# A four-layer gated kernel: routing and first weight loads moved within the first attention, and the shift of x moved to ScalarE in the competitive attention

## The chip, the cores and the metric

The kernel runs on one core of a Trainium2 chip. The metric is the device time of one execution in microseconds (us), as the median of several runs. A profile is the record of one such execution.

## What is computed

Four layers, each x + tanh(gate) * attention(layernorm(x), ctx), followed by x + tanh(gate) * ffn(layernorm(x)), over x of 32 batches x 128 rows x 128 and ctx of 32 x 77 x 128. The attention and the ffn differ from layer to layer. The change touches three of the eight:

```
# layer 0, attention: 16 heads, softmax over the 77 context rows
out = softmax(Q @ K.T / sqrt(8)) @ V @ Wo + bo
# layer 0, ffn: 2 of 8 experts for each row
probs = softmax(xf @ router_w.T); topv, topi = top_k(probs, 2); topv = topv / topv.sum()
out = sum over the two experts e: topv[e] * (gelu(xf @ w1[e]) @ w2[e])
# layer 1, attention: each row goes to its best context row
sim = sigmoid(beta + alpha * C @ X.T); mask = one_hot(argmax over context rows)
agg = (sim * mask) @ X + C; denom = mask.sum(rows) + 1.0
out = X + sim.T @ (agg / denom)
```

In the last line X is layernorm(x), so layer 1 adds gate * (X + ...) to x.

## The kernel before

The program is a row of phases (`nc.Block`), with a barrier of all engines between two. Within a phase each engine runs its own list of instructions in the order of the code, and semaphores tie the lists. Four arrays stay in SBUF throughout: x (32 batches, 128 rows on the partitions), its moments, the context and its transpose.

**`head_attention`, layer 0.** A software pipeline `pipeline4` over the 32 batches: in one step one batch is in its front (transposes, projections), another in its middle (exp, sum, scaling), another in its back (transposes of the probabilities, product with V), another in its tail (statistics of the new x). Per step VectorE sums the exponentials (L608), takes the reciprocal (L611, `softmax_recip`), and GpSimd scales 4 x 4 heads with it (L439), on which TensorE's transposes wait. Once 12 of the first 16 batches are through, the same phase routes the first half (16 batches) of the layer's own ffn beside the attention, in unrolled steps: moments and normalisation of x to `r.xn` in four groups of four batches (L576, at the `NORMALISE_STEPS` 15, 16, 17 and 19), their transposes on TensorE (L693), logits, exp at step 21 (`EXP`), `pick_first` and `pick_second` (top two experts), counts on TensorE, `rank_pairs` (place of each row in its expert's list), `slots_of_pairs`, `weigh_experts`, `expert_of_tiles` (which expert each tile of sorted rows belongs to). From step 25 (`SCATTER`) GpSimd issues, ahead of its scaling, three indirect DMAs a step (L431) that scatter 128 rows each into `sorted_x` in DRAM. There are 32, and those left go out in the last step, after its scaling. SP loads later weights and clears the scratch in this phase (to L410).

**`sparse_experts`, layer 0.** The sorted rows come in 2 halves of 20 tiles of 256 rows. SP loads for each tile two blocks of 256 KB of up weights (L926, L927, `load_weights`; the expert's number is read from `r.expert`) and 128 KB of rows (L935, `load_rows`) into buffers that are six deep (`DEPTH`); the first three tiles' weights come first, then the first three tiles' rows. TensorE transposes the rows (L1179) and multiplies. Within the phase GpSimd scatters the second half's rows (L964), and the second half's loads wait for that.

**`competitive_attention`, layer 1.** Eight groups of four batches run through a pipeline of front, middle and back. ScalarE normalises the next group (L1392, four activations), copies its transpose (L1402), exponentiates (L1407, L1410) and copies the transposed sims (L1398). VectorE takes the reciprocal that ends the sigmoid (L1452), counts and averages the rows of the group before (L1458 to L1465), finds the best context row of each row (L1470 to L1477, products and reductions over 128x308) and updates x (L1482). GpSimd weighs the tokens (L1356), multiplies xn by the gate (L1360) and adds that to x (L1364). Beside it the second half of the layer 0 ffn is brought home: GpSimd gathers rows of `sorted_y` (L1346), three batches a step, and VectorE adds them to x with their weights (`combine`, L1429 and L1434). TensorE runs the aggregation (L1504), transposes the sims (L1509), transposes the next xn (L1515), takes the similarities (L1521) and the output (L1529).

The helper `chain` links VectorE's instructions by a semaphore; `MID` and `BACK` count its links in a step. `clear` has GpSimd reset the semaphores of the phase before.

## Time and profile before

| | us |
|---|---|
| median of three runs (lowest, highest) | 1668.2 (1667.2, 1670.81) |
| the profiled execution's own time | 1669.93 |
| its span | 1668.1 |
| first attention, as cut below | 238.40 (23.00 to 261.40) |
| expert phase, layer 0 | 191.20 (261.40 to 452.60) |
| competitive attention | 103.90 (452.60 to 556.50) |

Over the span TensorE is busy 1395.9 us, VectorE 1056.0, GpSimd 789.5 and ScalarE 695.9; TensorE's mean granted clock is 0.922 of full speed. The profile page gives these sums, the chain of waits and the costliest groups of instructions. The trace behind it can be asked for windows (busy time of each engine in a stretch), for groups by line, and for the timeline (each instruction with its start, its length and what released it). In all of them PE is TensorE, PEld its weight loads, DVE is VectorE, ACT is ScalarE, POOL is GpSimd, and SPq, ACTq, POOLq are those engines' DMA queues. "L431" is a line of the kernel, and names are those of the program's buffers.

### The profile page before, as it was taken

To read this page: it belongs to the slowest core of one execution; us is meant where nothing else is said; L and a number is where in the kernel's file an instruction comes from. 1 tells how busy PE (TensorE), PEld (TensorE's weight loads), DVE (VectorE), ACT (ScalarE), POOL (GpSimd) and SP (SyncE) were. 2 spreads that over 40 slices of the span, in tenths; PEclk is the share of its full clock that TensorE was granted. 3 is DMA by queue.
4 is the path that set the end of the run, shared out by engine and by line. 5 is a ranking of instruction groups with operands and counts; after the bars stand their busy time and mean duration, and the time that the engine had idled before them with its cause. 6 is when DMAs were issued, how large, how long until landed. Compare 5 with 4: busy or idle time off the path is not lost. (4 is left out here: it accounts for less than half of the span.)

```text
span 1668.1 us, 34024 instructions
## 1 busy us (share of the span) xinstructions
PE 1395.9 (84%) x10919; PEld 1117.9 (67%) x10919; DVE 1056.0 (63%) x2354; ACT 695.9 (42%) x1695; POOL 789.5 (47%) x1005
## 2 busy tenths in 40 slices
PE   4999774989656785999979986999999999687996
PEld 3777554989645454666645555787888787486984
DVE  4888761413389696999958883555565755263455
ACT  3676452323344332665544442445545544321121
...
DMA packets 96485, 100.02 MB, mean 60 GB/s; under 512 B 12149, under 2 KB 69677, under 8 KB 95726
## 3 DMA queue, kind: packets, MB, share of 16 engines
...
## 5 line engine op out<-in xcount | busy, mean ns | idle before, releaser
L439 POOL TENSOR_TENSOR exp_scores<-exp_scores,softmax_recip 128x308 f32<-128x308 f32 x256 | 181.9, 743 | 180.7 <-DVE softmax_recip L611 180.6
L633 PE MATMUL psum<-identity,exp_scores 128*77 128x128 f32 x1024 | 163.6, 285 | 38.8 <-POOL exp_scores L439 26.2
L1944 POOL TENSOR_TENSOR exp_scores_xattn<-exp_scores_xattn,softmax_recip_xattn 128x1640 f32<-128x1640 f32 x32 | 93.5, 2923 | 162.4 <-DVE softmax_recip_xattn L2117 162.4
L1201 PE MATMUL psum<-sorted_transposed_ffn,tile_weights_up_ffn 128*128 128x128 f32 x1280 | 165.7, 284 | 5.3 <-DVE sorted_transposed_ffn L1089 5.2
L633 PEld LDWEIGHTS psum<-identity,exp_scores 128*77 128x77 f32 x1024 | 122.1, 152 | 61.9 <-issue 29.4
L1201 PEld LDWEIGHTS psum<-sorted_transposed_ffn,tile_weights_up_ffn 128*128 128x128 f32 x1280 | 155.1, 198 | 12.2 <-DVE sorted_transposed_ffn L1089 11.6
L975 POOL DMA_INDIRECT gathered_rows_ffn<-sorted_y,slot_ffn x96 | 90.9, 947 | 105.7 <-DMA sorted_y<-expert_rows_ffn 47.1
L454 ACT COPY probs_transposed<-psum 77x512 f32<-77x512 f32 x192 | 111.3, 582 | 57.3 <-PE psum L633 55.3
L964 POOL DMA_INDIRECT sorted_x<-xn_ffn,slot_ffn x64 | 61.5, 961 | 141.2 <-DVE slot_ffn L851 122.4
L1211 PE MATMUL psum<-expert_weights_down_ffn,hidden_ffn 128*128 x960 | 124.5, 281 | 3.4 <-issue 2.9
L1211 PEld LDWEIGHTS psum<-expert_weights_down_ffn,hidden_ffn 128*128 128x128 f32 x960 | 116.8, 197 | 5.3 <-issue 5.2
L1993 ACT ACTIVATE exp_scores_xattn<-psum,scaled_negated_max_xattn 128x205 f32<-128x205 f32 x256 | 106.6, 451 | 0.0
L2184 PE MATMUL psum<-kv_transposed_xattn,queries_xattn 128*128 128x205 f32 x512 | 97.8, 346 | 3.4 <-DVE queries_xattn L2122 3.4
L1004 ACT ACTIVATE hidden_ffn<-psum 128x512 f32<-128x512 f32 x80 | 47.7, 597 | 119.0 <-PE psum L1201 119.0
L536 DVE TENSOR_REDUCE negated_max<-psum 128x16 bf16<-128x1232 f32 (+1 forms) x64 | 90.8, 1419 | 4.5 <-PE psum L668 4.5
L2184 PEld LDWEIGHTS psum<-kv_transposed_xattn,queries_xattn 128*128 128x128 f32 x512 | 90.8, 196 | 4.0 <-DVE queries_xattn L2122 3.9
L1971 ACT COPY kv_transposed_xattn<-psum 128x205 f32<-128x205 f32 x32 | 10.6, 332 | 191.5 <-PE psum L2197 191.5
L1733 POOL TENSOR_TENSOR pick_ffn<-pick_ffn,descending_count 128x512 f32<-128x512 f32 x32 | 52.4, 1638 | 73.8 <-DVE pick_ffn L1800 73.8
L1089 DVE COPY sorted_transposed_ffn<-psum 128x256 f32<-128x256 f32 x80 | 33.7, 421 | 81.5 <-PE psum L1179 81.4
L2064 DVE TENSOR_REDUCE negated_max_xattn<-psum 128x4 f32<-128x820 f32 x64 | 64.7, 1011 | 25.3 <-PE psum L2184 24.9
L1119 DVE COPY expert_rows_ffn<-psum 128x256 f32<-128x256 f32 x80 | 34.0, 425 | 73.0 <-PE psum L1211 68.3
L502 ACT ACTIVATE exp_scores<-psum 128x1232 f32<-128x1232 f32 x64 | 76.7, 1198 | 6.1 <-PE psum L704 3.3
...
## 6 DMA issues: line engine op xcount, KB each, us to landing
...
sorted_x<-xn_ffn,slot_ffn POOLq DMA_INDIRECT x128, 2.2
gathered_rows_ffn<-sorted_y,slot_ffn POOLq DMA_INDIRECT x128, 2.7
```

Source lines behind the costliest of these rows:

```text
L439: nc.gpsimd.tensor_tensor(e[:, par, heads, :], e[:, par, heads, :], rec.to_broadcast([S, HG, KC]), ALU.mult).then_inc(s["probs_ready"], 1)
L454: nc.scalar.copy(pt[:, g * HG:(g + 1) * HG, :], m.psum[0:KC, 4 + g % 2, :].rearrange("p (h s) -> p h s", s=S)).then_inc(pt_read[g], 1)
L502: nc.scalar.activation(e[:, par, :, :].rearrange("p (j h) k -> p j (h k)", h=HG), m.psum[:, 0:NG, 0:HG * KC], ACT.Exp, scale=DK ** -0.5).t ...
L536: nc.vector.tensor_reduce(per_row(negmax, par), scores_view(), AX.XY if over_heads else AX.X, ALU.max, negate=True).then_inc(s["negmax_rea ...
L633: last = nc.tensor.transpose(m.psum[0:KC, 4 + g % 2, h * S:(h + 1) * S], e[:, nxt, g * HG + h, :], m.ident[:, :])
L975: nc.gpsimd.indirect_dma_start(yg[:, n % 4, k, :], None, m.sorted_y[half][:, :], bass.IndirectOffsetOnAxis(slot[:, half, k, b:b + 1], 0)). ...
L1201: mm = nc.tensor.matmul(m.psum[:, 2 * (n % 2) + half, to:to + SUB], w[:, n % DEPTH, u, at:at + 128], xst[:, n % 2, u * SUB:(u + 1) * SUB], ...
L1211: mm = nc.tensor.matmul(m.psum[:, 4 + n % 2, u * D:(u + 1) * D], hid[:, n % 2, c, u * 128:(u + 1) * 128], columns(n, u, c * D), start=(c = ...
L1944: nc.gpsimd.tensor_tensor(ev, ev, recip[:, par, :].unsqueeze(2).to_broadcast([S, H3, KV]), ALU.mult).then_inc(s["probs_ready"], 1)
L1993: ins = nc.scalar.activation(e[:, par, h, :], m.psum[:, h // HB, (h % HB) * KV:(h % HB + 1) * KV], ACT.Exp, scale=SCALE, bias=shift_bias[: ...
L2064: nc.vector.tensor_reduce(negmax[:, par, heads].rearrange("p (n h) -> p n h", h=HB), sv, AX.X, ALU.max, negate=True).then_inc(s["negmax_re ...
L2184: mm = nc.tensor.matmul(m.psum[:, h // HB, (h % HB) * KV:(h % HB + 1) * KV], q[:, par, h, :], kvt[:, par, :], start=True, stop=True)
```

## The change

It has three parts.

A. In the first attention the four normalisations go from VectorE to ScalarE, as activations with scale and bias. `COUNT` is one step earlier; `pick_second` stands in step 22 behind the reciprocal of that step (it had step 23 ahead of the sum), `rank_pairs` in step 23, `slots_of_pairs` also in step 23 behind the reciprocal (it had step 25), `weigh_experts` in 24, `expert_of_tiles` in 25, and scattering begins in step 24.

B. The buffer of the up weights and the semaphores `tile_loaded` outlive the phases; SP loads the up weights of the first six tiles within the attention, once the tiles' experts are known, and begins the expert phase of layer 0 with six loads of rows.

C. In the competitive attention, GpSimd's two instructions on x are gone. ScalarE instead scales and shifts x in place, four activations a group: x * (1 + gate * rstd) + gate * shift, with the two columns made on VectorE by `moves`. The division by the count moves from VectorE's product over the context rows to ScalarE's copy of the transposed sims, now four activations with a scale, behind the copy of xt. VectorE's order is interleaved anew, with `combine` ahead of the update of x; TensorE's sim transposes stand ahead of the aggregation.

```diff
-    PICK, COUNT = EXP + 1, EXP + 3
+    PICK, COUNT = EXP + 1, EXP + 2
...
@@ sync, first attention
+                    sync.wait_ge(s["route_known"], 1)
+                    for n in range(DEPTH):
+                        for u in range(TILE // SUB):
+                            e = sync.value_load(r.expert[0:1, 0, n * 2 + u:n * 2 + u + 1], min_val=0, max_val=E0 - 1)
+                            sync.dma_start(r.w_up[:, n, u, :], r.packed[bass.ds(e, 1), :, 0:F0].rearrange("o p c -> p (o c)")).then_inc(m.tile_loaded[r.layer][n], 16)
@@ scalar, first attention
+                    if at in NORMALISE_STEPS:
+                        g = NORMALISE_STEPS.index(at)
+                        act.wait_ge(s["route_shift"], 1 if g < PGROUPS - 1 else 2)
+                        for n in range(g * GB, (g + 1) * GB):
+                            ins = nc.scalar.activation(r.xn[:, n, :], m.x[:, n, :], ACT.Identity, scale=m.rstd2[:, n:n + 1], bias=m.shift2[:, n:n + 1])
+                        ins.then_inc(s["route_xn"], 1)
@@ vector, first attention
-                    if at in NORMALISE_STEPS:
...
-                    if at == PICK + 1:
-                        pick_second(nc, m, r, 0, link, s["route_picked"])
...
                     if at == COUNT + 1:
-                        slots_of_pairs(nc, m, r, 0, link, s["route_ranked"])
+                        weigh_experts(nc, m, r, 0, link)
                     if at == COUNT + 2:
-                        weigh_experts(nc, m, r, 0, link)
-                    if at == COUNT + 3:
                         expert_of_tiles(nc, m, r, 0, link, s["route_known"])
...
                         nc.vector.reciprocal(recip[:, par, :], total[:, par, :]).then_inc(s["recip_ready"], 1)
+                    if at == PICK:
+                        pick_second(nc, m, r, 0, link, s["route_picked"])
+                    if at == COUNT:
+                        slots_of_pairs(nc, m, r, 0, link, s["route_ranked"])
@@ sync, sparse_experts
-                for n in range(3):
-                    load_weights(n)
-                for n in range(3):
+                early = DEPTH if layer == 0 else 3
+                if layer == 3:
+                    for n in range(early):
+                        load_weights(n)
+                for n in range(early):
                     load_rows(n)
@@ gpsimd, competitive_attention
-                        wait(pool, s["x_moved"], g)
-                        nc.gpsimd.tensor_tensor(gated[:, :], xn[:, par, :, :].rearrange("p b d -> p (b d)"), m.gate[:, 1:2].to_broadcast([S, GB * D]),
-                                                ALU.mult).then_inc(s["xn_used"], 1)
-                        wait(pool, s["xn_used"], g + 1)
-                        xg = m.x[:, bass.ds(g * GB, GB), :].rearrange("p b d -> p (b d)")
-                        nc.gpsimd.tensor_tensor(xg, xg, gated[:, :], ALU.add).then_inc(s["x_moved"], 1)
@@ scalar, competitive_attention
                         ins.then_inc(s["xn_ready"], 1)
-                    if back:
-                        wait(act, s["simt_in_psum"], g)
-                        wait(act, s["y_done"], g - 1)
-                        nc.scalar.copy(simt[:, :], m.psum[0:KC, 2, :]).then_inc(s["simt_ready"], 1)
+                        wait(act, s["xn_ready"], g + 2)
+                        for t in range(GB):
+                            at = (g + 1) * GB + t
+                            ins = nc.scalar.activation(m.x[:, at, :], m.x[:, at, :], ACT.Identity, scale=move_scale[:, bass.ds(at, 1)],
+                                                       bias=move_shift[:, bass.ds(at, 1)])
+                        ins.then_inc(s["x_moved"], 1)
                     if front:
...
                         nc.scalar.copy(xt[:, nxt, :], m.psum[:, 0, :]).then_inc(s["xt_ready"], 1)
+                    if back:
+                        wait(act, s["simt_in_psum"], g)
+                        wait(act, s["y_done"], g - 1)
+                        wait(act, s["back_link"], (g - 1) * BACK + 2)
+                        for t in range(GB):
+                            ins = nc.scalar.activation(simt[:, t * S:(t + 1) * S], m.psum[0:KC, 2, t * S:(t + 1) * S], ACT.Identity,
+                                                       scale=tally[:, t // 2, t % 2:t % 2 + 1])
+                        ins.then_inc(s["simt_ready"], 1)
@@ vector, competitive_attention
+                def moves(lo, hi):
+                    nc.vector.tensor_scalar(move_scale[:, lo:hi], m.rstd[:, lo:hi], gate, 1.0, ALU.mult, ALU.add).then_inc(s["moves_ready"], 1)
+                    nc.vector.tensor_scalar(move_shift[:, lo:hi], m.shift[:, lo:hi], gate, None, ALU.mult).then_inc(s["moves_ready"], 1)
...
-                        wait(dve, s["back_link"], (g - 1) * BACK + 3)
-                        nc.vector.tensor_tensor(rows[:, :, :], rows[:, :, :], tl.unsqueeze(2).to_broadcast([KC, GB, D]), ALU.mult)\
-                            .then_inc(s["back_link"], 1)
...
+                    if g >= 0:
+                        combine(g)
                     if back:
                         wait(dve, s["y_done"], g)
                         wait(dve, s["x_moved"], g)
...
-                    if g >= 0:
-                        combine(g)
@@ tensor, competitive_attention
                     if back:
+                        wait(pe, s["sim_ready"], g)
+                        wait(pe, s["simt_ready"], g - 1)
+                        for t in range(GB):
+                            mm = nc.tensor.transpose(m.psum[0:KC, 2, t * S:(t + 1) * S], sim[:, nxt, t, :], m.ident[:, :])
+                        mm.then_inc(s["simt_in_psum"], 1)
                         wait(pe, s["pick_ready"], g)
```

How the instructions stand at three places, before and with the change (an instruction's line, kind, what it writes <- reads, the shape it writes, how many). First GpSimd at the end of the first attention, from the scaling of the last step but three. Before:

```order
L439 TENSOR_TENSOR exp_scores<-exp_scores,softmax_recip 128x308 x4
L424 TENSOR_TENSOR x_residual<-x_residual,L_bo_row 128x128
L431 DMA sorted_x<-xn_ffn,slot_ffn 5120x128 x3
L439 TENSOR_TENSOR exp_scores<-exp_scores,softmax_recip 128x308 x4
L431 DMA sorted_x<-xn_ffn,slot_ffn 5120x128 x3
L439 TENSOR_TENSOR exp_scores<-exp_scores,softmax_recip 128x308 x4
L431 DMA sorted_x<-xn_ffn,slot_ffn 5120x128 x11
L398 UNCONDITIONAL_BRANCH
```

With the change:

```order
L445 TENSOR_TENSOR exp_scores<-exp_scores,softmax_recip 128x308 x4
L430 TENSOR_TENSOR x_residual<-x_residual,L_bo_row 128x128
L437 DMA sorted_x<-xn_ffn,slot_ffn 5120x128 x3
L445 TENSOR_TENSOR exp_scores<-exp_scores,softmax_recip 128x308 x4
L437 DMA sorted_x<-xn_ffn,slot_ffn 5120x128 x3
L445 TENSOR_TENSOR exp_scores<-exp_scores,softmax_recip 128x308 x4
L437 DMA sorted_x<-xn_ffn,slot_ffn 5120x128 x8
L399 UNCONDITIONAL_BRANCH
```

Eleven scatters stood behind the last scaling, now eight do; three are issued a step earlier at the front.

Second, SP from the last loads of the first attention into the expert phase. Before:

```order
L410 DMA expert_weights_down_ffn<-in_L_ffn_packed_dram 128x512 x8
L398 UNCONDITIONAL_BRANCH
L911 UNCONDITIONAL_BRANCH
L926 TENSOR_LOAD tile_expert_ffn
L926 ISA x2
L927 ISA
L927 DMA tile_weights_up_ffn<-in_L_ffn_packed_dram 128x512
```

With the change, the end of the twelve loads and what follows:

```order
L415 TENSOR_LOAD tile_expert_ffn
L415 ISA x2
L416 ISA
L416 DMA tile_weights_up_ffn<-in_L_ffn_packed_dram 128x512
L399 UNCONDITIONAL_BRANCH
L919 UNCONDITIONAL_BRANCH
L943 DMA sorted_rows_ffn<-sorted_x 128x2x128 x6
```

The weight loads of the first six tiles (each with a register load ahead of it) stand before the branch that ends the attention, and the phase begins with rows.

Third, ScalarE in one step of the competitive attention. Before:

```order
L1392 ACTIVATE xn_xattn<-x_residual,x_shift,x_rstd 128x128 x4
L1398 COPY sim_transposed_xattn<-psum 77x512
L1402 COPY xt_xattn<-psum 128x512
L1407 ACTIVATE sim_xattn<-psum,minus_alpha_beta_xattn 128x308
L1410 ACTIVATE sim_xattn<-sim_xattn,one 128x308
```

With the change:

```order
L1395 ACTIVATE xn_xattn<-x_residual,x_shift,x_rstd 128x128 x4
L1401 ACTIVATE x_residual<-x_residual,gated_shift_xattn,one_plus_gated_rstd_xattn 128x128 x4
L1407 COPY xt_xattn<-psum 128x512
L1413 ACTIVATE sim_transposed_xattn<-psum,token_count_xattn 77x128 x4
L1420 ACTIVATE sim_xattn<-psum,minus_alpha_beta_xattn 128x308
L1423 ACTIVATE sim_xattn<-sim_xattn,one 128x308
```

Four activations on x come in ahead of the copy of xt, and the transposed sims, now four activations, move behind it.

## Rows read from the trace of the kernel before

**Rows 1.** Windows by stage: engines' busy us (count), TensorE's clock, DMA share, GB/s

```profile
261.40:452.60 191.20, 163.39 (x1410) 161.61 (x1410) 64.32 (x191) 56.09 (x92) 61.04 (x64) 0.93 0.64 188
452.60:556.50 103.90, 59.36 (x256) 51.91 (x256) 87.17 (x190) 40.31 (x77) 62.26 (x57) 0.53 0.07 21
```

**Rows 2.** Timeline, end of the first attention: start, us, engine, instruction [idle<-releaser]

```profile
257.50 0.96 POOL L431 DMA_INDIRECT sorted_x<-xn_ffn,slot_ffn  x1 [0.30 <-issue]
261.43 0.21 DVE L316 TENSOR_TENSOR x_mean_doubled<-x_moments 128x32 f32<-128x32 f32 x1 [12.36 <-PEq L398]
```

**Rows 3.** Timeline of GpSimd in the first attention, steps 25 and 26

```profile
196.28 1.19 POOL L431 DMA_INDIRECT sorted_x<-xn_ffn,slot_ffn  x1 [2.72 <-DVE slot_ffn L851]
200.08 2.66 POOL L439 TENSOR_TENSOR exp_scores<-exp_scores,softmax_recip 128x308 f32<-128x308 f32 x4
207.61 2.67 POOL L439 TENSOR_TENSOR exp_scores<-exp_scores,softmax_recip 128x308 f32<-128x308 f32 x4 [0.52 <-DVE softmax_recip L611]
```

**Rows 4.** Timeline of the first attention where one group is normalised and transposed

```profile
120.67 1.31 ACT L454 COPY probs_transposed<-psum 77x512 f32<-77x512 f32 x2
121.28 1.12 DVE L576 TENSOR_SCALAR xn_ffn<-x_residual,x_second_rstd,x_second_shift 128x128 f32<-128x128 f32 x4
123.14 0.65 PE L693 MATMUL psum<-identity,xn_ffn 128*128 128x128 f32 x4
```

**Rows 5.** Timeline, start of the expert phases of layers 0 and 3

```profile
262.35 6.32 SPq L927 DMA_DIRECT2D tile_weights_up_ffn<-in_L_ffn_packed_dram  x6
268.71 1.46 SPq L935 DMA_DIRECT2D sorted_rows_ffn<-sorted_x  x3
272.26 0.69 PE L1179 MATMUL psum<-identity,sorted_rows_ffn 128*128 128x128 f32 x2 [23.91 <-DMA sorted_rows_ffn<-sorted_x]
...
1444.70 0.21 DVE L316 TENSOR_TENSOR x_mean_doubled<-x_moments 128x32 f32<-128x32 f32 x1 [0.31 <-PEq L1915]
1444.96 0.34 SPq L915 DMA_DIRECT2D shared_w_up_ffn<-in_L_ffn_Ws_dram  x1
```

**Rows 6.** Timeline of the expert phase of layer 0, start of its second half

```profile
318.03 0.96 POOL L964 DMA_INDIRECT sorted_x<-xn_ffn,slot_ffn  x1 [59.58 <-DVE slot_ffn L851]
...
359.51 0.38 SPq L935 DMA_DIRECT2D sorted_rows_ffn<-sorted_x  x1
361.74 0.69 PE L1179 MATMUL psum<-identity,sorted_rows_ffn 128*128 128x128 f32 x2 [6.30 <-DMA sorted_rows_ffn<-sorted_x]
```

**Rows 7.** Groups of the competitive attention: busy us, mean ns | idle us before<-releaser

```profile
L1452 DVE RECIPROCAL sim_xattn<-sim_xattn 128x308 f32<-128x308 f32 x8 | 16.5, 2065 | 7.8 <-ACT sim_xattn L1410 7.8
L1477 DVE TENSOR_TENSOR pick_xattn<-pick_xattn,pick_code_xattn 128x308 f32<-128x308 f32 x8 | 11.6, 1444 | 0.3
L1475 DVE TENSOR_TENSOR pick_xattn<-pick_xattn,descending_count 128x308 f32<-128x308 f32 x8 | 8.5, 1065 | 0.3
L1465 DVE TENSOR_TENSOR context_out_xattn<-context_out_xattn,token_count_xattn 77x512 f32<-77x512 f32 x8 | 5.5, 687 | 0.3
L1398 ACT COPY sim_transposed_xattn<-psum 77x512 f32<-77x512 f32 x8 | 4.6, 578 | 19.6 <-PE psum L1509 19.6
```

**Rows 8.** Timeline of the competitive attention, ScalarE's and VectorE's

```profile
455.28 1.63 ACT L1392 ACTIVATE xn_xattn<-x_residual,x_shift,x_rstd 128x128 f32<-128x128 f32 x4
458.12 0.59 ACT L1402 COPY xt_xattn<-psum 128x512 f32<-128x512 f32 x1 [1.20 <-PE psum L1515]
...
465.24 0.48 DVE L1475 TENSOR_TENSOR pick_xattn<-pick_xattn,descending_count 128x308 f32<-128x308 f32 x1
468.87 2.14 DVE L1429 SCALAR_TENSOR_TENSOR x_residual<-gathered_rows_ffn,expert_weight_ffn,x_residual 128x128 f32<-128x128 f32 x4
470.94 1.13 DVE L1434 SCALAR_TENSOR_TENSOR x_residual<-gathered_rows_ffn,expert_weight_ffn,x_residual 128x128 f32<-128x128 f32 x4
...
502.44 1.20 DVE L1475 TENSOR_TENSOR pick_xattn<-pick_xattn,descending_count 128x308 f32<-128x308 f32 x1
```

**Rows 9.** DMA issues of the page: engine op xcount, median us to landing

```profile
gathered_rows_ffn<-sorted_y,slot_ffn POOLq DMA_INDIRECT x128, 2.7
```

51 lines of the change are left out of this document (26 added, 25 removed).

## The prediction

> **What bounds the kernel now.** I read the windows by stage first, then the timeline at the three seams the change touches. The kernel is a row of phases with a barrier between them, and three of them change, so each is costed by its own last wait. In the expert phase TensorE is busy 163.39 of 191.20 us, in the competitive attention no engine is: VectorE has 87.17 of 103.90 us, and TensorE's granted clock is 0.53, all but at the lower of its two levels, 1.2 GHz [rows 1]. The first attention ends with GpSimd: after the last two steps' scalings eleven scatters are left, the last of them at 257.50, and VectorE has been idle 12.36 us when the next phase starts at 261.43 [rows 2]. Ahead of that stands one stall: GpSimd has waited 2.72 us for the slots when it scatters at 196.28, and the scaling that step 25 needs starts only behind the three scatters, at 200.08; afterwards the step is GpSimd's own, 7.5 us to 207.61, of which it waits 0.52 [rows 3]. In the expert phase TensorE's first matmul waits until 272.26, last for rows whose load SP issued only at 268.71, after 6.32 us of weight loads [rows 5].
>
> **Part A, routing in fewer steps: 3.6 us less.** Scattering starts one step earlier, so three of the eleven scatters at the tail move into the loop. A scatter takes 0.96 and 0.30 of issue [rows 2], 1.26; three are 3.8 us. What do they cost where they go? In step 24 GpSimd issues three that it did not issue there. But the stall of step 25 goes: the slots are now made in step 23, so that step 24's scatters find them ready, and step 25's scaling no longer waits for slots and then for three scatters (2.72 + 3 x 1.26 = 6.5 us of GpSimd's time; six scatters need 7.6, and its idle time in step 24 takes the rest). Followed step by step the scaling of step 25 comes at 200.2 against 200.08, with three more scatters behind it, and from there on the step is the same. VectorE gets `pick_second`, `rank_pairs` and the slots into steps 22 and 23, behind the reciprocal that GpSimd waits for where it can be; GpSimd has 4 us of room there. **The normalisation** leaves VectorE (four instructions, 1.12 us, from 121.28 [rows 4]) for ScalarE. The price there is that of the like activations in the competitive attention, four in 1.63 us [rows 8]. TensorE transposes this tile at 123.14 [rows 4], right behind work that ends there. ScalarE copies the step's last probabilities until 121.98 [rows 4], would be done at 123.6, and queues the next copy of xt behind it; so TensorE waits up to 0.5, while VectorE's next reduction comes 1.1 sooner. That happens in four steps: I take 0.2 lost in all, between a gain of 1.1 and a loss of 2.0. So A is 3.8 - 0.2 = 3.6, bounds 1.5 to 5.
>
> The Trainium skill ("ScalarE: Activation LUTs", "Rules for kernel authors") speaks against this: it says that adds and multiplies belong on VectorE, not on ScalarE. The two rows agree with it in size, 1.63 against 1.12 for four tiles; if the rule alone counted, the four moved groups would cost 4 x 0.5 = 2.0 us rather than 0.2 and the time would be 1.8 above my figure.
>
> **Part B, first weights loaded within the attention: 7.6 us less.** SP's twelve loads there follow its weight loads of the phase, which it finished long before; they run while GpSimd scatters, and a scatter takes the same 0.96 us in the expert phase with DMA at a share of 0.64 over the phase [rows 1, 6], so I cost them at nothing (without that cover, 12 x 1.05 = 12.6 us of SP time, the 6.32 us row twice). What goes is the 6.32 us of loads ahead of the rows. In the other expert phase SP issues its first load 0.26 us after VectorE's first instruction [rows 5]; by that the rows start at 261.7 instead of 268.71. They need 3.55 us to land here (268.71 to 272.26, behind six weight loads) [rows 5] and 2.2 in the second half (359.51 to 361.74) [rows 6]. So TensorE starts between 263.9 and 265.2 rather than 272.26: 7.0 to 8.4, and I take 7.6. Is it carried to the end of the phase? The second half's scatters (32, from 318.03) start when tile 7 is under way, which moves with the start, and the wait for them at 361.74 moves as well; nothing there is tied to another clock. Below I allow 6.5.
>
> **Part C, competitive attention: 5.0 us less.** VectorE loses the multiply of context rows by the count: 5.5 us (8 x 687 ns) [rows 7]. It also loses company. The two products of 128x308 take 1065 and 1444 ns on average, yet the first took 0.48 us where GpSimd was not at work (at 465.24) [rows 7, 8]: (585 + 964) x 8 = 12.4 us, and four instructions of `combine` took 2.14 against the 1.13 of the next four [rows 8], 1.0 more. Of GpSimd's three wide products two go (gated xn, x add); `weighted_tokens` stays, and where it alone ran beside a product that took 1.20 (at 502.44) [rows 8], so 0.72 x 8 = 5.8 us stays. Freed on VectorE: 5.5 + 12.4 + 1.0 - 5.8 = 13.1.
>
> Given back, step by step along the new order:
> - At the start the x shift (1.63 us) stands ahead of the first copy of xt, which waited 1.20 for TensorE [rows 8]: +0.45.
> - `combine` moves ahead of the update of x. A gather lands in 2.7 us [rows 9], and the update and the statistics covered about 2.0 of it in the first step: +2.0.
> - Four small instructions (`moves`, two pairs, some 0.2 each by the first instruction of a phase [rows 2]): +0.8.
> - ScalarE now has eight activations and a copy between two sigmoids, 1.63 + 1.63 + 0.6, and for `sim_transposed` four at 1.45 by estimate (a little under xn's 1.63) where there was one copy, 0.58 by the group's mean [rows 7]. In the later steps, without gathers, VectorE already waited for ScalarE (7.8 us before the reciprocals [rows 7]); there the saving of some 0.9 a step in three steps is not had, and one is 0.6 longer: +3.3.
> - At the end four transposes, 0.65 us near the full clock [rows 4] and some 1.05 at this phase's, stand ahead of the last aggregation, and nothing hides them: +1.05.
>
> Together 7.6, so 5.5 remain; following the steps one by one (old reciprocals at 462.11, 472.77 ... 541.71) gave 3.8 to 4.8. I take 5.0, bounds 1 and 9.
>
> **Sum.** 3.6 + 7.6 + 5.0 = 16.2 from the profiled execution's 1669.93 us: 1653.7. That execution lay 1.7 above the median of 1668.2 (span 1668.1); by the median 1652.0.
>
> **Rivals.**
> 1. Part C gives nothing: the gather's wait and ScalarE's longer chain swallow it. For it speaks that 7.8 us of VectorE's idle time already waits for ScalarE; against it that VectorE is at 84% in this phase. 1668.2 - 11.2 = 1657.0.
> 2. Part B gives half, as the first six row loads are late behind the barrier or the weights are still landing: 1652.0 + 3.8 = 1655.8. Against it: the loads have some 50 us.
> 3. Part C gives the 13.1 us whole, as the gathers have landed and ScalarE keeps up: 1652.0 - 8.1 = 1643.9.
> 4. Slower: ScalarE becomes the loop. If the x shift (8 x 1.63 = 13.0), the longer `sim_transposed` (8 x 0.87 = 7.0) and the normalisation (4 x 1.63 = 6.5) all stand in series with VectorE, 26.5 us are added, while A and B still give 11.4: 1668.2 + 26.5 - 11.4 = 1683.3. It decides once ScalarE's work in a competitive step, now about 5.0 (40.31 us in 8 steps [rows 1]) and then some 7.5, passes the step's 12 us or lies wholly between sigmoid and reciprocal. The first is far off; the second holds only in the last steps. The Trainium skill's rule above points this way, though by it alone the change would be only 1.8 us dearer.
> 5. The change doesn't do what it says: if the scatters stayed where they are (slots still late), A is 0: 1655.6.
>
> **How the numbers follow.** Forecast 0.55, rival 1 0.20, rivals 2 and 5 0.12 together, rival 3 0.09, rival 4 0.04. No more than 2 in 10 is left out if the range holds the forecast and rivals 1, 2 and 5 with 2 us beyond, and below the better half of the way to rival 3: 1647.5 to 1659.0. A measurement here can tell about 0.2%, 3.3 us: every case but rival 4 is faster by more, and 0.03 is for a mixture of all losses. Faster 0.93, same 0.03, slower 0.04.
>
> **What would show it.** In the new profile: the last scatter of the attention some 3.8 us earlier, no wait of GpSimd for the slots; first matmul of the expert phase at 260 to 262; the competitive phase about 99 us long, 128x308 products at 0.5 and 0.7 to 1.2 us, gated xn gone, waits for the gather in the first step and for ScalarE in the last ones. I am wrong if TensorE in the attention waits for ScalarE's normalisation in more than two steps, if the first rows land later than 265, or if VectorE's idle time in the competitive attention grows by more than what its busy time loses.

## The result, and the profile after

The changed kernel takes 1645.9 us (median of four runs, 1645.2 to 1647.34) against 1668.1 for the kernel before in the same comparison: a ratio of 0.9868, with a 95% interval of 0.9856 to 0.9881, so 22 us less. The forecast was 1652.0 with a range of 1647.5 to 1659.0: the direction held, the size did not, and the time lies 1.6 us below the range. The profiled execution took 1646.58 us, its span is 1644.8. One execution of the version without part B, below, took 2336.12 us at a granted clock of 0.555; that version's median and ratio leave it out.

The seams of the phases, in the timeline of the changed kernel (start, duration, engine, line, instruction [idle before <- what ended it]); they answer to [rows 2, 5]:

```profile
255.07 0.96 POOL L437 DMA_INDIRECT sorted_x<-xn_ffn,slot_ffn  x1 [0.30 <-issue]
258.94 2.96 SPq L943 DMA_DIRECT2D sorted_rows_ffn<-sorted_x  x6
259.00 0.21 DVE L317 TENSOR_TENSOR x_mean_doubled<-x_moments 128x32 f32<-128x32 f32 x1 [8.34 <-PEq L399]
...
261.85 0.69 PE L1189 MATMUL psum<-identity,sorted_rows_ffn 128*128 128x128 f32 x2 [11.90 <-DMA sorted_rows_ffn<-sorted_x]
...
441.01 0.17 DVE L1431 TENSOR_SCALAR minus_alpha_beta_xattn<-L_alpha_beta 128x2 f32<-128x2 f32 x1 [6.71 <-PEq L918]
...
533.45 0.21 DVE L317 TENSOR_TENSOR x_mean_doubled<-x_moments 128x32 f32<-128x32 f32 x1 [0.30 <-PEq L1344]
```

And of the kernel before, the first instruction of VectorE in the competitive attention and in the phase behind it:

```profile
452.65 0.17 DVE L1418 TENSOR_SCALAR minus_alpha_beta_xattn<-L_alpha_beta 128x2 f32<-128x2 f32 x1 [6.70 <-PEq L910]
...
556.58 0.21 DVE L316 TENSOR_TENSOR x_mean_doubled<-x_moments 128x32 f32<-128x32 f32 x1 [0.30 <-PEq L1334]
```

| stretch | before | after | difference | forecast |
|---|---|---|---|---|
| start to VectorE's first instruction of the expert phase | 261.43 | 259.00 | -2.4 | -3.6 (A) |
| from there to TensorE's first matmul | 10.83 | 2.85 | -8.0 | -7.6 (B) |
| from there to the competitive attention | 180.39 | 179.16 | -1.2 | 0 |
| competitive attention | 103.93 | 92.44 | -11.5 | -5.0 (C) |
| rest of the span | 1111.5 | 1111.35 | -0.2 | 0 |

Parts A and B came out within 1.2 us of the forecast; part C gave more than twice as much. The window of the competitive attention in the changed kernel (length, then busy us of TensorE, its weight loads, VectorE, ScalarE and GpSimd, then TensorE's clock, DMA share, GB/s):

```profile
441.01:533.45 92.44, 55.35 (x256) 49.17 (x256) 71.11 (x189) 56.66 (x133) 42.19 (x41) 0.57 0.09 23
```

The same window in the kernel before:

```profile
452.65:556.58 103.93, 59.36 (x256) 51.91 (x256) 87.17 (x190) 40.31 (x77) 62.26 (x57) 0.53 0.07 21
```

VectorE's busy time fell by 16.1 us and its idle time grew from 16.8 to 21.3, by 4.6; the difference is the 11.5. ScalarE took on 16.4 us, GpSimd lost 20.1. Some groups of VectorE and ScalarE there in the changed kernel (busy us, mean ns | idle before):

```profile
L1413 ACT ACTIVATE sim_transposed_xattn<-psum,token_count_xattn 77x128 f32<-77x128 f32 x32 | 9.0, 359 | 15.7 <-DVE token_count_xattn L1485 15.7
...
L1505 DVE SCALAR_TENSOR_TENSOR x_residual<-psum,tanh_gates,x_residual 128x512 f32<-128x512 f32 x8 | 5.9, 742 | 7.4 <-PE psum L1551 7.4
L1496 DVE TENSOR_TENSOR pick_xattn<-pick_xattn,descending_count 128x308 f32<-128x308 f32 x8 | 5.7, 713 | 0.0
...
L1448 DVE SCALAR_TENSOR_TENSOR x_residual<-gathered_rows_ffn,expert_weight_ffn,x_residual 128x128 f32<-128x128 f32 x16 | 4.8, 344 | 2.1 <-DMA gathered_rows_ffn<-sorted_y,slot_ffn 2.1
...
L1498 DVE TENSOR_TENSOR pick_xattn<-pick_xattn,pick_code_xattn 128x308 f32<-128x308 f32 x8 | 4.0, 505 | 0.3
```

The two products of 128x308 cost 713 and 505 ns on average, not 1065 and 1444 [rows 7]; the waits that grew are the gather's 2.1 us and the 7.4 us for TensorE's output ahead of the update of x. The group of that update in the kernel before had 4.7:

```profile
L1482 DVE SCALAR_TENSOR_TENSOR x_residual<-psum,tanh_gates,x_residual 128x512 f32<-128x512 f32 x8 | 5.9, 742 | 4.7 <-PE psum L1529 4.7
```

For ScalarE's sigmoid VectorE waited once in this phase, ahead of the first reciprocal, before and after alike; the 7.8 us of [rows 7] are this one wait:

```profile
462.11 2.08 DVE L1452 RECIPROCAL sim_xattn<-sim_xattn 128x308 f32<-128x308 f32 x1 [7.75 <-ACT sim_xattn L1410]
```

```profile
450.79 2.08 DVE L1472 RECIPROCAL sim_xattn<-sim_xattn 128x308 f32<-128x308 f32 x1 [7.67 <-ACT sim_xattn L1423]
```

### The profile page after: what moved, and what is told of

The parts are those of the page before. It is cut to its first block and busy times, and to the rows that moved or that the text cites. A ratio compares the mean times of both kernels' runs of the same rounds, so it can differ in the third digit from the quotient of the medians.

```text
span 1644.8 us, 34070 instructions
## 1 busy us (share of the span) xinstructions
PE 1391.0 (85%) x10919; PEld 1114.0 (68%) x10919; DVE 1037.0 (63%) x2336; ACT 716.7 (44%) x1767; POOL 768.4 (47%) x989
## 5 line engine op out<-in xcount | busy, mean ns | idle before, releaser
L1211 PEld LDWEIGHTS psum<-sorted_transposed_ffn,tile_weights_up_ffn 128*128 128x128 f32 x1280 | 153.8, 197 | 11.7 <-DVE sorted_transposed_ffn L1099 11.5
L640 PEld LDWEIGHTS psum<-identity,exp_scores 128*77 128x77 f32 x1024 | 122.5, 152 | 56.7 <-issue 26.3
```

Of the source, the lines that this page charges most:

```text
L640: last = nc.tensor.transpose(m.psum[0:KC, 4 + g % 2, h * S:(h + 1) * S], e[:, nxt, g * HG + h, :], m.ident[:, :])
L1211: mm = nc.tensor.matmul(m.psum[:, 2 * (n % 2) + half, to:to + SUB], w[:, n % DEPTH, u, at:at + 128], xst[:, n % 2, u * SUB:(u + 1) * SUB], ...
```

## The experiments

Each one starts from the changed kernel, except the first, which starts from the kernel before. All times are medians. The profiles show that stretches with the same code differ from one to the next: the first attention of the kernel before ended at 261.43, in the next experiment, with the same code there, at 260.47, and the unchanged rest behind the competitive attention took between 1106.4 and 1112.8 us over all profiles. TensorE's 6958 matmuls in that rest were busy for 968.0 to 976.9 us, and the rest is long where they are (c_alone 1112.8 and 976.9 us, pick_late_shift_last 1106.7 and 968.2); what makes them differ, the runs don't settle. So each effect is read from its own stretch within one profile, and the total stands beside it. In the competitive attention alone the six profiles with the changed kernel's code there (the changed kernel's, c_alone, without_a, without_b, normalise_on_vector, pick_late) have 92.40 to 93.34 us, so a difference under 1 us there is read from its steps. Step 0 is the one that starts with the first reciprocal of the sigmoid.

**Part C alone.** The edits of `competitive_attention`, as the change's diff has them, on the kernel before; of its lines:

```diff
-                        nc.gpsimd.tensor_tensor(xg, xg, gated[:, :], ALU.add).then_inc(s["x_moved"], 1)
...
+                moves(0, B - HBATCH)
...
+                    if g >= 0:
+                        combine(g)
                     if back:
                         wait(dve, s["y_done"], g)
```

> The kernel before with part C alone. If the three parts simply add, the competitive attention takes some 92.4 us as in the changed kernel (before: 103.9) and the time is 11.5 us under before, 1656.6. Rival: part of C's gain rests on B (persistent semaphores, so that GpSimd clears fewer and gathers earlier) or on A; then the phase is 94 us or longer and the time 1658 to 1663, towards the 5.0 us of the forecast.

Measured: 1657.9 us, ratio 0.9935 (0.9919 to 0.9952). The first instruction of VectorE in the phase and behind it, in its timeline:

```profile
451.17 0.17 DVE L1421 TENSOR_SCALAR minus_alpha_beta_xattn<-L_alpha_beta 128x2 f32<-128x2 f32 x1 [6.70 <-PEq L910]
...
543.57 0.21 DVE L316 TENSOR_TENSOR x_mean_doubled<-x_moments 128x32 f32<-128x32 f32 x1 [0.30 <-PEq L1334]
```

It is 92.40 us long; with A and B it is 92.44, and within 1 us of that in the other profiles with this code. C's gain is its own: nothing of it above 1 us rests on A or B. The total, 10.4 us under the 1668.2 of its comparison, lies between the two theories; the phase decides.

**Without part B.** The twelve loads in the attention go, and the expert phase begins as before.

```diff
-                early = DEPTH if layer == 0 else 3
-                if layer == 3:
...
+                for n in range(3):
+                    load_weights(n)
+                for n in range(3):
                     load_rows(n)
```

> The changed kernel without part B: the first weights are loaded in the expert phase again, rows behind them. If B is worth its earlier start alone, TensorE's first matmul comes 8.0 us later after VectorE's first instruction of the phase (10.8 against 2.85) and the time is 1653.9. Rival: B also gives 1.2 us later in the phase (the whole phase shrank by 9.2), then 1655.1.

Measured: 1654.4 us, ratio 0.9919 (0.99 to 0.9939). In its timeline, the start of the expert phase:

```profile
259.14 0.21 DVE L316 TENSOR_TENSOR x_mean_doubled<-x_moments 128x32 f32<-128x32 f32 x1 [6.01 <-PEq L398]
...
270.06 0.69 PE L1180 MATMUL psum<-identity,sorted_rows_ffn 128*128 128x128 f32 x2 [17.64 <-DMA sorted_rows_ffn<-sorted_x]
```

TensorE starts 10.92 us behind VectorE's first instruction instead of 2.85: B is worth 8.07 us there. From TensorE's start to the competitive attention this kernel takes 178.8 us, c_alone 179.8, the changed kernel 179.2 and the kernel before 180.4; kernels with and without B lie on both sides, so the 1.2 us of the table is not B's, but belongs to what differs from run to run. The rival falls with it.

**Without part A.** The edits of `head_attention` on routing and normalisation taken back.

```diff
-    PICK, COUNT = EXP + 1, EXP + 2
+    PICK, COUNT = EXP + 1, EXP + 3
...
+                    if at == PICK + 1:
+                        pick_second(nc, m, r, 0, link, s["route_picked"])
...
                     if at == COUNT + 1:
-                        weigh_experts(nc, m, r, 0, link)
+                        slots_of_pairs(nc, m, r, 0, link, s["route_ranked"])
...
-                    if at == PICK:
-                        pick_second(nc, m, r, 0, link, s["route_picked"])
-                    if at == COUNT:
-                        slots_of_pairs(nc, m, r, 0, link, s["route_ranked"])
```

> The changed kernel without part A: routing and normalisation as before, with eleven scatters behind the last scaling. By the new profile A gave 2.4 us at the end of the attention (the forecast said 3.6): 1648.3, or 1649.5 by the forecast. Rival: A gave nothing beyond what differs from run to run, some 1 us; then 1646 to 1647.

Measured: 1647.5 us, ratio 0.9883 (0.9867 to 0.99), 1.6 above the changed kernel. Its timeline, from the reciprocal of step 22 to VectorE's first instruction of the next phase:

```profile
174.10 0.25 DVE L617 RECIPROCAL softmax_recip<-softmax_sum 128x16 f32<-128x16 f32 x1
...
262.16 0.22 DVE L317 TENSOR_TENSOR x_mean_doubled<-x_moments 128x32 f32<-128x32 f32 x1 [12.25 <-PEq L399]
```

That stretch is 88.1 us, 87.6 in the kernel before, 87.5 in c_alone and 84.8 in the changed one; over the eight profiles that route as the changed kernel does, it is 84.8 to 85.6. Behind step 22 A gives 2 to 3 us, less than the 3.8 of three scatters. The total lies between the theory and the rival; this stretch decides for the theory.

**The normalisation back on VectorE.**

```diff
-                            ins = nc.scalar.activation(r.xn[:, n, :], m.x[:, n, :], ACT.Identity, scale=m.rstd2[:, n:n + 1], bias=m.shift2[:, n:n + 1])
+                            ins = nc.vector.tensor_scalar(r.xn[:, n, :], m.x[:, n, :], m.rstd2[:, n:n + 1], m.shift2[:, n:n + 1], ALU.mult, ALU.add)
```

> The changed kernel with the four normalisations of the routing back on VectorE. By the forecast's sum the move to ScalarE lost 0.2 us (between a gain of 1.1 and a loss of 2.0), so 1645 to 1647 and the phase's end within 1 us of 259.0. If ScalarE's 0.5 us a group were exposed in each step, the attention ends 2 us earlier, 1644. If VectorE bound these steps, it ends up to 2 us later, 1648.

Measured: 1644.4 us (1642.7 to 1648.35), ratio 0.9852 (0.9829 to 0.9875); the attention ends at 258.84 against 259.00. The total tells no difference; the steps do. From the reciprocal of step 13 to that of step 22, a stretch with all four normalisations in it, the four profiles with them on VectorE (this one, the kernel before, c_alone, without_a) have 63.72 to 63.76 us, the ten with them on ScalarE 63.76 to 63.78. So the move costs under 0.1 us. Within the stretch much shifts: against this kernel the changed one gains 1.03, 0.26 and 1.03 us in three of the steps and loses 0.21, 1.30 and 0.84 in three others. TensorE waits for ScalarE in each of the four steps, 1.5 us in all; the first in the timeline of the changed kernel:

```profile
123.91 0.66 PE L700 MATMUL psum<-identity,xn_ffn 128*128 128x128 f32 x4 [0.37 <-ACT xn_ffn L521]
```

**The second pick later.**

```diff
+                    if at == COUNT:
+                        pick_second(nc, m, r, 0, link, s["route_picked"])
                     if back:
                         wait(dve, s["pt_in_psum"], (b - 1) * NG + 2)
...
-                    if at == PICK:
-                        pick_second(nc, m, r, 0, link, s["route_picked"])
                     if at == COUNT:
                         slots_of_pairs(nc, m, r, 0, link, s["route_ranked"])
```

> The changed kernel with the second pick moved within the first attention from behind the reciprocal of step 22 to behind the normalisation of x in step 23, where VectorE waits 1.46 us. Theory 1 (the pick, 3.05 us where GpSimd's scaling runs beside it, holds up the negated maximum that TensorE waits 3.09 us for, and the whole step with it): the reciprocal of step 23 comes 2 us earlier and so does the end of the attention; 1644. Theory 2 (GpSimd's scatters bound the steps behind it and take the gain away): the attention ends where it did, 1646. Rival: counting waits for the later pick, and the slots come too late for step 24, a loss of 1 to 3 us.

Measured: 1643.7 us, ratio 0.9851 (0.9833 to 0.9869). The timeline of the changed kernel from the reciprocal of step 22 to that of step 23:

```profile
174.18 0.25 DVE L614 RECIPROCAL softmax_recip<-softmax_sum 128x16 f32<-128x16 f32 x1
...
175.39 0.67 DVE L802 TENSOR_TENSOR pick_ffn<-pick_ffn,descending_count 128x128 f32<-128x128 f32 x1
...
176.80 0.67 DVE L812 TENSOR_TENSOR picked_either_ffn<-pick_ffn 128x128 bf16<-128x128 f32 x1
...
177.60 1.42 DVE L548 TENSOR_REDUCE negated_max<-psum 128x16 bf16<-128x1232 f32 x1
...
179.07 1.21 PE L711 MATMUL psum<-negated_max,identity_bf 128*128 128x308 bf16 x4 [3.09 <-DVE negated_max L548]
...
186.63 0.25 DVE L614 RECIPROCAL softmax_recip<-softmax_sum 128x16 f32<-128x16 f32 x1
```

The same stretch with the pick later, and VectorE's first instruction behind the attention:

```profile
172.93 0.25 DVE L616 RECIPROCAL softmax_recip<-softmax_sum 128x16 f32<-128x16 f32 x1
...
173.25 1.42 DVE L548 TENSOR_REDUCE negated_max<-psum 128x16 bf16<-128x1232 f32 x1
...
174.73 0.71 PE L711 MATMUL psum<-negated_max,identity_bf 128*128 128x308 bf16 x4
...
182.84 0.25 DVE L616 RECIPROCAL softmax_recip<-softmax_sum 128x16 f32<-128x16 f32 x1
...
256.08 0.21 DVE L317 TENSOR_TENSOR x_mean_doubled<-x_moments 128x32 f32<-128x32 f32 x1 [8.54 <-PEq L399]
```

In the changed kernel the second pick runs from 174.34 to 177.47, beside GpSimd's scaling, and its 128x128 products take up to 0.67 us in the lines above; only then comes the negated maximum that TensorE has waited 3.09 us for, and the next reciprocal follows 12.45 us behind the last. With the pick later the two are 9.91 apart, and from the reciprocal to the end of the attention it is 83.15 us instead of 84.82. Of the 2.5 us 1.7 reach the end; theory 1. In the next step 0.7 us go: from its reciprocal at 182.84 to the one behind takes 8.78 us here and 8.05 in the changed kernel, with TensorE's granted clock at 0.62 and 1.00 over the 9 us from that reciprocal. Kernels with the changed kernel's code in this phase show both lengths, 8.05 at 1.00 (combine_last) and 8.79 at 0.81 (without_b), so this loss need not be the later pick's.

**The context rows ahead.**

```diff
-                    if middle:
-                        wait(dve, s["sim_ready"], g + 1)
-                        wait(dve, s["weighted_ready"], g - 1)
-                        nc.vector.tensor_reduce(best[:, par, :], sv, AX.X, ALU.max).then_inc(s["best_ready"], 1)
                     if back:
                         wait(dve, s["back_link"], (g - 1) * BACK + 1)
                         nc.vector.reciprocal(tl, tl).then_inc(s["back_link"], 1)
...
-                        link_m(nc.vector.tensor_tensor(pv, sv, best[:, par, :].unsqueeze(2).to_broadcast(wide), ALU.is_ge))
                     if back:
                         wait(dve, s["y_done"], g - 1)
...
+                    if middle:
+                        wait(dve, s["sim_ready"], g + 1)
+                        wait(dve, s["weighted_ready"], g - 1)
+                        nc.vector.tensor_reduce(best[:, par, :], sv, AX.X, ALU.max).then_inc(s["best_ready"], 1)
...
+                        link_m(nc.vector.tensor_tensor(pv, sv, best[:, par, :].unsqueeze(2).to_broadcast(wide), ALU.is_ge))
```

The addition of the context rows stands in the second `if back`.

> The changed kernel with VectorE's order in the competitive attention partly as before: the addition of the context rows stands ahead of the best-row reduction, so that the 128x308 products follow it directly. Theory 1 (the order did it: other instructions now stand beside GpSimd's weighted tokens): the two products rise from 0.71 and 0.51 us to about 1.2 and 0.7, 8 x 0.7 = 5 us on VectorE, the phase is 95 to 98 us and the time 1649 to 1651. Theory 2 (only the number of GpSimd's products counts): they stay within 0.1 us, the time is 1646 to 1647.

Measured: 1646.0 us, ratio 0.9869 (0.9853 to 0.9886). The group of the first product:

```profile
L1496 DVE TENSOR_TENSOR pick_xattn<-pick_xattn,descending_count 128x308 f32<-128x308 f32 x8 | 9.7, 1208 | 0.3
```

The phase's window:

```profile
440.83:534.15 93.32, 53.37 (x256) 46.91 (x256) 74.82 (x188) 56.73 (x133) 41.85 (x41) 0.61 0.08 23
```

Both theories are half right. The order does keep the product away from GpSimd's weighted tokens: put back, it costs 1208 ns instead of 713, and VectorE is 3.7 us busier. But the phase is only 0.9 us longer, since VectorE waits 2.8 us less elsewhere. And of that 0.9 us belongs to TensorE's clock: ahead of the last update of x its eight output matmuls took 1.13 us here, at a granted clock of 1.00, and 2.05 at 0.50 in the changed kernel. Without that the order is worth 1.8 us of the phase: steps 2, 4 and 6 are 0.78, 0.70 and 0.68 longer, step 7 is 0.35 shorter.

**The shift back on GpSimd.**

```diff
-                            ins = nc.scalar.activation(m.x[:, at, :], m.x[:, at, :], ACT.Identity, scale=move_scale[:, bass.ds(at, 1)],
...
+                        nc.gpsimd.tensor_tensor(gated[:, :], xn[:, par, :, :].rearrange("p b d -> p (b d)"), m.gate[:, 1:2].to_broadcast([S, GB * D]),
+                                                ALU.mult).then_inc(s["xn_used"], 1)
...
+                        nc.gpsimd.tensor_tensor(xg, xg, gated[:, :], ALU.add).then_inc(s["x_moved"], 1)
```

> The changed kernel with GpSimd's two products on x back in place of ScalarE's four activations, VectorE's new order kept. Theory 1 (order and number both count): VectorE's products beside them rise to 1 us or more each, the phase is 97 to 101 us, the time 1650 to 1654. Theory 2 (the number of GpSimd's products is all): the two products cost 1.07 and 1.44 us as before, the phase 100 to 103 us, the time 1653 to 1656. Rival: ScalarE's longer chain costs as much as the contention did; then the time stays within 1 us of 1646.

Measured: 1653.1 us, ratio 0.9913 (0.9897 to 0.993). Groups of `combine` and of the second product:

```profile
L1450 DVE SCALAR_TENSOR_TENSOR x_residual<-gathered_rows_ffn,expert_weight_ffn,x_residual 128x128 f32<-128x128 f32 x16 | 10.0, 671 | 2.2 <-DMA gathered_rows_ffn<-sorted_y,slot_ffn 2.2
...
L1500 DVE TENSOR_TENSOR pick_xattn<-pick_xattn,pick_code_xattn 128x308 f32<-128x308 f32 x8 | 8.8, 1100 | 0.3
```

The phase's window:

```profile
442.33:542.46 100.13, 55.90 (x256) 48.67 (x256) 80.73 (x189) 44.17 (x101) 61.87 (x57) 0.59 0.08 21
```

The phase is 7.7 us longer and VectorE 9.6 busier, now mostly in the second product (505 to 1100 ns) and in `combine` (344 to 671 ns): with the new order GpSimd's products run into other instructions, which pay the same. This is the largest single part of C. The phase and the time lie where the two theories overlap; the products decide for theory 1, for the first took 530 ns and the second 1100, not 1065 and 1444 as before.

**The division back on VectorE.**

```diff
-                        for t in range(GB):
-                            ins = nc.scalar.activation(simt[:, t * S:(t + 1) * S], m.psum[0:KC, 2, t * S:(t + 1) * S], ACT.Identity,
-                                                       scale=tally[:, t // 2, t % 2:t % 2 + 1])
-                        ins.then_inc(s["simt_ready"], 1)
+                        nc.scalar.copy(simt[:, :], m.psum[0:KC, 2, :]).then_inc(s["simt_ready"], 1)
...
+                        nc.vector.tensor_tensor(rows[:, :, :], rows[:, :, :], tl.unsqueeze(2).to_broadcast([KC, GB, D]), ALU.mult)
```

> The changed kernel with the division by the count back on VectorE: a product over the context rows there, one plain copy of the transposed sims on ScalarE. Theory 1 (costs on VectorE count in the early steps only, in the last three steps VectorE waits for ScalarE and TensorE): 8 x 0.69 = 5.5 us more on VectorE of which the four early ones and the last reach the end, 2 to 4 us: phase 94.5 to 96.5, time 1648 to 1650. Theory 2 (VectorE bounds every step): 5.5 us, 1651.4. Rival (ScalarE bounds, its copy is shorter by 0.55 a step): no loss, 1646 or less.

Measured: 1650.1 us (1644.29 to 1652.77), ratio 0.9889 (0.9871 to 0.9908). The phase's window:

```profile
439.19:535.33 96.14, 56.48 (x256) 50.10 (x256) 76.49 (x196) 52.30 (x109) 43.59 (x41) 0.61 0.09 22
```

VectorE is 5.4 us busier and the phase 3.7 longer: theory 1. TensorE's clock differs from the changed kernel's at two places and about cancels: the output matmuls took 2.07 us instead of 1.13 in step 6, and 1.16 instead of 2.05 ahead of the last update.

**Combine behind the update of x.**

```diff
-                    if g >= 0:
-                        combine(g)
                     if back:
                         wait(dve, s["y_done"], g)
...
+                    if g >= 0:
+                        combine(g)
```

> The changed kernel with combine back behind the update of x and its statistics. Theory 1 (the wait for the gather of step 1, 2.15 us, is bare only because combine stands ahead): the wait falls to 0.6 us or less, but in the other steps with gathers VectorE now waits for TensorE's output ahead of combine (0.8 us in one step, up to 2 in two more), so the phase lies between 91 and 95 us, the time between 1644.5 and 1648.5. Theory 2 (the forecast's term, 2.0 us, is wholly given back by this order): phase 90.4, time 1643.9. Rival: GpSimd's gathers, which wait for combine, come later and stretch the steps with gathers; phase above 95 us.

Measured: 1649.6 us, ratio 0.989 (0.9874 to 0.9907), slower than any of the theories but the rival had it, though not by the rival's way. The phase's window:

```profile
440.55:536.74 96.19, 57.70 (x256) 51.39 (x256) 72.59 (x188) 56.67 (x133) 41.77 (x41) 0.57 0.08 22
```

The group of the update of x:

```profile
L1503 DVE SCALAR_TENSOR_TENSOR x_residual<-psum,tanh_gates,x_residual 128x512 f32<-128x512 f32 x8 | 6.0, 749 | 11.8 <-PE psum L1551 11.8
```

The update of step 3 in the timeline:

```profile
489.31 0.75 DVE L1503 SCALAR_TENSOR_TENSOR x_residual<-psum,tanh_gates,x_residual 128x512 f32<-128x512 f32 x1 [2.98 <-PE psum L1551]
```

In the changed kernel the timeline has in step 3 `combine`, its statistics and the update:

```profile
486.89 0.87 DVE L1448 SCALAR_TENSOR_TENSOR x_residual<-gathered_rows_ffn,expert_weight_ffn,x_residual 128x128 f32<-128x128 f32 x3
487.68 0.87 DVE L1453 SCALAR_TENSOR_TENSOR x_residual<-gathered_rows_ffn,expert_weight_ffn,x_residual 128x128 f32<-128x128 f32 x3
488.47 0.67 DVE L1458 BATCH_NORM_STATS2 x_moments<-x_residual 128x6 f32<-128x128 f32 x3
489.97 0.75 DVE L1505 SCALAR_TENSOR_TENSOR x_residual<-psum,tanh_gates,x_residual 128x512 f32<-128x512 f32 x1 [0.83 <-PE psum L1551]
```

Step 1 did get 1.33 us shorter (from one reciprocal of the sigmoid to the next), as the gather is waited for no more. But steps 2, 3 and 4 got 1.14, 2.15 and 0.97 longer. In step 3 TensorE's output comes late: VectorE waits 2.98 us for it, where in the changed kernel it does the three rows of `combine` first and waits 0.83. In steps 2 and 4 the second 128x308 product meets GpSimd (1.83 and 0.74 us), and in step 4 TensorE's output is 0.60 late. Another 0.83 goes in step 6, where TensorE's eight output matmuls take 2.05 us, at a granted clock of 0.50, instead of 1.13 at 1.00. That need not be `combine`'s doing: without_b and pick_late, with the changed kernel's code in this phase, have the same step 6, 7.65 and 7.66 us against 7.65 here and 6.82 in the changed kernel. In all the phase is 96.19 us, 3.75 longer, 2.9 without that step, and VectorE's waits for TensorE's output are 11.8 us instead of 7.4.

**The shift of x last.**

```diff
-                        wait(act, s["xn_ready"], g + 2)
-                        for t in range(GB):
-                            at = (g + 1) * GB + t
-                            ins = nc.scalar.activation(m.x[:, at, :], m.x[:, at, :], ACT.Identity, scale=move_scale[:, bass.ds(at, 1)],
-                                                       bias=move_shift[:, bass.ds(at, 1)])
-                        ins.then_inc(s["x_moved"], 1)
                     if front:
                         nc.scalar.copy(xt[:, nxt, :], m.psum[:, 0, :]).then_inc(s["xt_ready"], 1)
...
                         nc.scalar.activation(sv, sv, ACT.Identity, bias=m.one[:, 0:1]).then_inc(s["one_added"], 1)
+                        wait(act, s["xn_ready"], g + 2)
+                        for t in range(GB):
+                            at = (g + 1) * GB + t
+                            ins = nc.scalar.activation(m.x[:, at, :], m.x[:, at, :], ACT.Identity, scale=move_scale[:, bass.ds(at, 1)],
+                                                       bias=move_shift[:, bass.ds(at, 1)])
+                        ins.then_inc(s["x_moved"], 1)
```

> The changed kernel with ScalarE's scale and shift of x behind the sigmoid instead of ahead of the copy of xt. Theory 1 (in the last steps and at the start the shift stands in the chain by what remains of it once TensorE has transposed, some 0.4 us): 0.4 us at each of four places, phase 91, time 1644.3. Theory 2 (the shift is fully hidden behind TensorE's transposes): no change, 1646. Rival: the shift now delays the next step's xn by up to 1.65 us where ScalarE has no idle time; then slower by 1 to 3 us.

Measured: 1642.9 us, ratio 0.9841 (0.9822 to 0.986); the phase is 89.81 us. At its start ScalarE's timeline has the copy of xt behind xn, after 1.21 us of waiting for TensorE, and no shift between:

```profile
443.96 1.63 ACT L1395 ACTIVATE xn_xattn<-x_residual,x_shift,x_rstd 128x128 f32<-128x128 f32 x4
446.80 0.59 ACT L1401 COPY xt_xattn<-psum 128x512 f32<-128x512 f32 x1 [1.21 <-PE psum L1537]
```

The first reciprocal comes 0.35 us earlier, and the steps that end in ScalarE's chain shrink by 0.37 each (9.54 instead of 9.91, twice): theory 1, at three places rather than four. That is 1.1 us. Step 0 is 0.67 shorter too, since a product meets GpSimd less, but c_alone and without_b, with the shift ahead, have 8.22 us there against 8.15 here and 8.82 in the changed kernel, so this need not be the shift's. The other 0.93 is at the end of the phase, where the last eight output matmuls ran at the upper of TensorE's two levels, 2.4 GHz. The window over them:

```profile
527.90:529.20 1.30, 1.13 (x8) 0.97 (x8) 0.01 (x1) 1.28 (x2) 0.00 (x0) 1.00 0.00 0
```

The window over the same eight in the changed kernel, at the lower level, 1.2 GHz:

```profile
529.30:531.50 2.20, 2.05 (x8) 1.78 (x8) 0.01 (x1) 1.49 (x3) 0.00 (x0) 0.50 0.00 0
```

TensorE had waited 1.75 us before them in both. rows_ahead, scale_on_vector and pick_late_shift_last had the full clock there too; three_moves, with the shift last, had the half. So 0.9 us between two such kernels can be the clock's.

**The second pick late and the shift last.** Both edits at once.

> The changed kernel with the second pick late and ScalarE's shift of x behind the sigmoid, both at once. They lie in different phases; if they add, 1.7 us less in the attention and 2.6 less in the competitive attention, 1641.6. Rival: something that both feed, such as the gathers or a DMA, takes one of them back; then 1643 to 1644.

Measured: 1639.5 us (1636.58 to 1642.09), ratio 0.9836 (0.982 to 0.9852); the changed kernel had 0.9868 (0.9856 to 0.9881). The phase's window shows it as short as with the shift alone:

```profile
438.21:528.07 89.86, 55.03 (x256) 48.35 (x256) 70.49 (x188) 56.41 (x133) 42.15 (x41) 0.59 0.09 24
```

From the reciprocal of step 22 to the end of the attention it takes 82.6 us, as with the pick alone or a little less. So the two add: 2.2 and 2.6 us in the stretches that they touch, 0.9 of it the clock of the last matmuls. The medians differ by 6.4 us, and much of that is not the edits': in the two profiles, 10.0 us apart, 4.6 lie in the unchanged rest, at 1106.7 us near the low end of what the profiles show. This version beats both kernels, but by less than its time says.

**Combine behind the update in step 1 alone, on top of these two.**

```diff
-                    if g >= 0:
+                    if g >= 0 and g != 1:
                         combine(g)
...
+                    if g == 1:
+                        combine(g)
```

> The kernel with the second pick late and the shift of x last, and besides combine behind the update of x in step 1 alone. Theory 1 (combine ahead pays in the other steps, as it fills VectorE's wait for TensorE's output, and costs in step 1, where it waits 2.15 us for a gather): step 1 gets 1.3 us shorter as it did with combine behind the update throughout, the rest stays, the phase is 88.5 us and the time 1.3 us under the version with two moves, 1638.2. Theory 2 (combine in step 1 sets when GpSimd gathers for the next steps): the 1.3 us come back in steps 2 and 3 and the time stays at 1639.5.

Measured: 1645.7 us, ratio 0.986 (0.9843 to 0.9877), a loss against the version with two moves, and by neither theory. In the timeline of step 1, the end of ScalarE's sigmoid, its next xn and VectorE's update:

```profile
457.15 0.55 ACT L1417 ACTIVATE sim_xattn<-sim_xattn,one 128x308 f32<-128x308 f32 x1
...
459.15 1.63 ACT L1395 ACTIVATE xn_xattn<-x_residual,x_shift,x_rstd 128x128 f32<-128x128 f32 x4
...
466.44 0.75 DVE L1505 SCALAR_TENSOR_TENSOR x_residual<-psum,tanh_gates,x_residual 128x512 f32<-128x512 f32 x1 [3.43 <-PE psum L1553]
```

With the shift behind the sigmoid, xn of step 1 begins at 459.15, 1.45 us behind the sigmoid's end, so TensorE's output comes later too, and VectorE waits 3.43 us for it. `combine` was what filled that time; step 1 takes 12.36 us instead of 11.22 in the version with two moves. The 1.33 us were to be had only with the shift ahead. The last steps lose another 1.5 us with the output matmuls at the lower clock, and 5.2 of the 9.9 us between that version's profile and this one lie in the unchanged rest.

## Why the prediction was right or wrong

**Part A: right in kind, up to 1.2 us too large.** The three scatters left the tail, and GpSimd's wait for the slots went. What failed is the sentence that GpSimd has 4 us of room behind the reciprocal, so that `pick_second` costs nothing there. Who waited was TensorE, for the negated maximum queued behind the pick on VectorE; the step grew to 12.45 us, and step 25's scaling came at 202.04, not 200.2. pick_late took the pick away and got 1.7 us; the three profiles with the late pick have 82.6 to 83.2 us behind step 22, at least 4.4 below any without A: with the pick out of TensorE's way A gives more than the 3.6. The normalisation, booked at 0.2 us, cost under 0.1. TensorE's wait for it in four steps is by the prediction's own list a sign of being wrong; but its sum had such a wait in four steps too, and three other steps give as much back. The Trainium skill's rule ("ScalarE: Activation LUTs", "Rules for kernel authors"), for which the forecast had worked out 2.0 us, agrees with the instructions, 1.65 us for four tiles on ScalarE against VectorE's 1.12 [rows 4]; the time of the stretch shows none of it.

**Part B: right.** 8.0 us against 7.6: six row loads begin as VectorE starts, the first rows are there 2.9 us later, and the twelve loads in the attention, issued from 200.80 to 214.21, cost nothing that shows: scatters beside them took 0.96 to 1.03 us, against 0.96 to 1.04 in the kernel before.

**Part C: right in sign, wrong in size, by one term above all.** The sum booked `combine`'s new place as a loss of 2.0 us, for the gather of step 1. The gather's wait is there, 2.15 us in step 1. But combine_last shows what the same place is worth in the other steps: the phase without that move is 96.19 us, with it 92.44, a gain of 3.75, of which 0.83 is TensorE's clock in step 6 and 2.9 the move's. Without the move the forecast's sum would have been 5.0 + 2.0 = 7.0, and that version gained 103.93 - 96.19 = 7.7. So the term was wrong by 4.9 of the 6.5 us that the phase was off (by 5.75 with the clock's part). The gather costs 1.33 us in step 1, where the update of x would otherwise wait 0.89 for TensorE. Against it stand 2.75 us in steps 3 and 4, where `combine` fills VectorE's wait for TensorE's output, and some 1.4 in steps 2 and 4, where with it the second product runs less beside GpSimd's weighted tokens. I had looked for what the moved block would wait for, and not for the wait that it now fills (TensorE's output is late in the step behind the statistics) nor for what it shifts away from GpSimd.

The other terms of C:
- *What stays of the contention*, 5.8 us, was 2.1 by the two products' means (713 + 505 - 960 ns, by 8): the new order keeps them away from the weighted tokens. But rows_ahead shows that this mis-sizing was worth 1.8 us in time at one clock (0.9 as measured), not 3.7. I had charged the steps twice, once for contention on VectorE and once (3.3 us) because VectorE waits there anyway; where it waits, contention cost nothing: in rows_ahead steps 3 and 5 are as long as in the changed kernel, with the product at 1.20 us instead of 0.59.
- *VectorE's wait for ScalarE in the later steps*, 3.3 us, rests on a misreading: the 7.8 us of [rows 7] are one wait at the start of the phase. In the later steps VectorE waited for TensorE's output, 1.27 us in each of two in the kernel before, 0.83, 2.99 and 0.74 us in three with the change. What ScalarE's longer chain costs by itself is not shown; its shift gives 0.37 in each of two steps (shift_last).
- *The multiply* freed 5.5 us of VectorE and 3.7 of the phase, *GpSimd's two products* 9.6 and 7.7. With the clock's part left out the parts sum to 7.7 + 3.7 + 2.9 + 1.8 = 16.1, more than 11.5: undone one by one each is measured against an order tuned to the rest, and what the longer work of ScalarE and TensorE's new order cost was not undone by itself.
- *The start* lost 0.32 against 0.45, and the shift there can be had for nothing (shift_last). ScalarE's four scaled copies took 1.13 us against my 1.45, so that it never became the loop: its 56.7 us busy stay under VectorE's 71.1.

Rival 3, in which C gives VectorE's whole 13.1 us, with a chance of 0.09 and a time of 1643.9, came nearest. It named the wrong reason, for the gather was waited for and VectorE's idle time did grow, by 4.6 us; what it got right is that most of what VectorE loses reaches the end.

What stays open: TensorE's swapped order in the competitive attention was not tried alone, nor was the position of `rank_pairs` and the slots.
